# Values of two steps together and a softmax in three parts, in a four-layer attention kernel

## The reference

```python
x = L0(x)   # channel attention: h = group_norm(x); q,k,v = W h + b; softmax(q k^T / sqrt(32)) v; x + proj
x = L1(x)   # one head over points: softmax(q^T k), value with 128 channels; x + gamma * Wo y
x = L2(x)   # 8 heads of 32 over 1024 points: h = group_norm(x); softmax(q^T k / sqrt(32)) v; x + proj
x = L3(x)   # the same with its own weights; the residual is the normalised x
```

## Time and profile before

| | |
|---|---|
| time, median of 3 runs | 2928.32 us (2926.51 to 2933.37) |
| the profiled execution's own time | 2925.99 us |
| its span, first to last instruction | 2924.2 us |
| PE busy | 2778.9 us, 95% |
| POOL busy | 2154.3 us, 74% |
| DVE busy | 1863.7 us, 64% |
| ACT busy | 1553.3 us, 53% |
| mean granted TensorE clock | 0.987 |

### The profile page before, as it was taken

How to read it: one execution, slowest core, us unless ns; L and a number is a source line. 1 busy time by engine, 2 the same in 40 slices (tenths; PEclk the granted TensorE clock), 3 DMA queues, 4 the chain that set the end, 5 groups by cost and what they waited for, 6 DMA issues and landing times.

```text
span 2924.2 us, 35836 instructions
## 1 busy us (share of the span) xinstructions
PE 2778.9 (95%) x12912; PEld 1379.1 (47%) x12912; DVE 1863.7 (64%) x3341; ACT 1553.3 (53%) x2794; POOL 2154.3 (74%) x740
## 2 busy tenths in 40 slices
PE   6879999999999999999999999999999999999998
PEld 4444445544455444554445445454445544444442
DVE  1347776576756667566675676756776566767672
ACT  2225655556555556455564555644655446566554
POOL 3208777688867788687886888858887688887877
PEclk9979999999999999999999999999999999999999
DMA  2060344303434145232450334413343313433340
GB/s 81 25 95 18 47 75 60 51 20 47 88 46 56 24 51 93 33 52 46 53 94 13 46 60 57 76 23 35 60 74 60 48 24 46 75 46 46 46 60 16
DMA packets 74387, 150.85 MB, mean 52 GB/s; under 512 B 9121, under 2 KB 10657, under 8 KB 74210
## 3 DMA queue, kind: packets, MB, share of 16 engines
q1 hardware_dynamic: 74210, 148.56, 33.2%
HBM read 20.46 MB, written 16.78 MB: 13 GB/s over the span
## 4 chain that ended last, share of the span: by engine, by line
PE 70%; ACT 9%; POOL 8%; DMA 6%; DVE 4%; issue 3%; SPq 0%; ACTq 0%; POOLq 0%; DVEq 0%
PE psum L1335 16%; PE psum L1360 12%; PE psum L1304 11%; PE psum L1243 6%; POOL vT L841 5%; PE psum L1274 5%; ACT prob L945 5%; PE psum L1251 4%; PE psum L1356 4%; DMA K<-hi 3%; DMA Q<-max_rows 2%; PE psum L1383 2%; PE psum L1178 2%; POOL acc L841 2%; PE psum L1378 1%
## 5 line engine op out<-in xcount | busy, mean ns | idle before, releaser
L1082 DVE TENSOR_REDUCE maxpart<-psum 128x1 f32<-128x512 f32 x2176 | 1407.1, 684 | 730.2 <-PE psum L1304 705.9
L945 ACT ACTIVATE prob<-psum 128x512 f32<-128x512 f32 x2176 | 1224.8, 596 | 921.9 <-PE psum L1335 886.7
L841 POOL TENSOR_TENSOR acc<-acc,prob 128x2048 f32<-128x2048 f32 (+1 forms) x317 | 1130.3, 3566 | 163.4 <-ACT prob L945 133.9
L1335 PE MATMUL psum<-Q,K 104*128 104x512 f32 x2048 | 1080.7, 529 | 69.4 <-ACT prob L945 41.5
L1304 PE MATMUL psum<-K,Q 96*128 96x512 f32 x2048 | 820.8, 404 | 15.1 <-DVE maxpart L1082 11.6
L1335 PEld LDWEIGHTS psum<-Q,K 104*128 104x128 f32 x2048 | 384.4, 188 | 765.7 <-ACT prob L945 473.9
L841 POOL TENSOR_TENSOR vT<-vT,prob 128x2048 f32<-128x2048 f32 x122 | 556.2, 4559 | 22.5 <-ACT prob L945 12.0
L1360 PE MATMUL psum<-prob,vT 128*32 128x512 f32 x4096 | 555.6, 604 | 0.0
L1304 PEld LDWEIGHTS psum<-K,Q 96*128 96x128 f32 x2048 | 391.9, 191 | 149.3 <-issue 72.4
L841 POOL TENSOR_TENSOR acc<-prob 128x2048 f32<-128x2048 f32 (+1 forms) x58 | 212.3, 3661 | 314.7 <-ACT prob L945 161.9
L1360 PEld LDWEIGHTS psum<-prob,vT 128*32 128x32 f32 x4096 | 97.2, 108 | 197.0 <-ACT prob L945 110.3
(11 more groups left out here) (138 smaller groups left out, 2070.5 us busy)
## 6 DMA issues: line engine op xcount, KB each, us to landing
Q<-hi SPq DMA_DIRECT2D x128, 256.0 KB
K<-hi SPq DMA_DIRECT2D x128, 256.0 KB
Q<-lo SPq DMA_DIRECT2D x64, 256.0 KB
K<-lo SPq DMA_DIRECT2D x64, 256.0 KB
scratch<-xa SPq DMA_DIRECT2D x8, 1024.0 KB, 4.0
xb<-scratch SPq DMA_DIRECT2D x8, 1024.0 KB, 4.8
xa<-in_x SPq DMA_DIRECT2D x7, 1024.0 KB, 8.6
out<-hb SPq DMA_DIRECT2D x7, 1024.0 KB, 5.8
```

The source lines that it names most:

```text
L841: pool.tensor_tensor(total, first if a == 1 else total, this, ALU.add).then_inc(added, 1)
L945: act.activation(prob[STEP_STARTS.slot(b, start)][:, j, :], score_bank[(SCORES.rank[b.n][e] - 1) % SCORE_BANKS], ACT.Exp, scale=1.0 if lay ...
L1082: dve.tensor_reduce(maxpart[layer][:, a // NQ, a % NQ:a % NQ + 1], bank, AX_X, ALU.max).then_inc(max_free, 1)
L1335: pe.matmul(score_bank[(r - 1) % SCORE_BANKS], left, right, start=True, stop=True).then_inc(score_full, 1)
```

## The change

1. The values of two steps are issued together in groups 2.2, 2.3 and 3.0 of the steady turns (`PAIRED`): at the last slot of an even step the values of the two steps before, and none at the last slot of an odd step. So values come at slots 3, 11, 19 and 27.
2. A finish waits in the plan for a slot with values, and invert and scale follow it by 2 and 5 slots, as before. After a paired group's slot 3 that makes finish 11, invert 13, scale 16.
3. Layer 0's softmax is three events: `softmax0` (maximum and subtraction on DVE), `exp0` (ACT), `scale0` (the rest on DVE), each with a slot of its own. In 2.2 there are 19 events spread over slots 12 to 30 instead of 17: rows 12 and 13, turn 14 to 17, gram 18 to 24, keys 25 and 26, logits with `softmax0` 27, `exp0` 28, `scale0` 29. `maxrow` at slot 27 comes behind the logits.
4. Layer 2's out pieces in 3.0 start at slot 20 instead of 16.

```diff
+PAIRED = {(2, 2), (2, 3), (3, 0)}
...
-    return ([("side", layer, "gram"), ("side", layer, "keys"), [("side", layer, "logits"), ("softmax0", layer)]]
+    return ([("side", layer, "gram"), ("side", layer, "keys"), [("side", layer, "logits"), ("softmax0", layer)], ("exp0", layer), ("scale0", layer)]
...
-            b += spread(12, end, side(0, "rows", 2) + side(0, "turn", KC // 2) + gram_to_logits)
+            b += spread(12, end, side(0, "rows", 2) + side(0, "turn", KC // 2) + gram_to_scale)
...
-             (1, 0, spread(0, 7, rest5[1:3]), [(1, 1, 0, 8, 0, 3), rows(1, 1, 6)]),
-             (1, 1, spread(0, 6, rest5[3:6]), []),
+             (1, 0, spread(0, 7, rest5[1:4]), [(1, 1, 0, 8, 0, 3), rows(1, 1, 6)]),
+             (1, 1, spread(0, 6, rest5[4:8]), []),
...
-              + [(3, 0, paced(0, 4, late3) + spread(SCALED, end, out2),
+              + [(3, 0, paced(0, 4, late3) + spread(SCALED + 4, end + 1, out2),
...
-            pending.extend((clock + after, (kind,) + x[1:3]) for kind, after in
-                           (("finish", FINISH_AFTER), ("invert", INVERT_AFTER), ("scale", SCALE_AFTER)))
+            pending.append((clock + FINISH_AFTER, ("finish",) + x[1:3]))
+
+    def finished(of, now):
+
+        for kind, after in (("invert", INVERT_AFTER), ("scale", SCALE_AFTER)):
+            pending.append((now + after - FINISH_AFTER, (kind,) + of))
+        pending.sort(key=lambda x: x[0])
...
+                paired = groups is turns[3] and (layer, g) in PAIRED
+                with_values = j == HPT - 1 and (s % 2 == 0 or not paired)
...
-                while pending and pending[0][0] <= clock:
+                while pending and pending[0][0] <= clock and (with_values or pending[0][1][0] != "finish"):
                     x = pending.pop(0)[1]
                     (turning if x[0] == "finish" else plan).append(x)
+                    if x[0] == "finish":
+                        finished(x[1:], clock)
...
-                while j == HPT - 1 and len(late) > LAG:
+                while with_values and len(late) > LAG:
                     advance(plan)
...
-    OWN = {"stats": 1, "norm": 1, "softmax0": 4, "split": 3, "invert": 1}
+    OWN = {"stats": 1, "norm": 1, "softmax0": 1, "scale0": 3, "split": 3, "invert": 1}
...
-                    elif e[0] == "softmax0":
-                        act.wait_ge(l0_ready, b.after(SOFTMAX0, e))
+                    elif e[0] == "exp0":
+                        act.wait_ge(l0_ready, b.after(SOFTMAX0, ("softmax0", e[1])))
...
-                        dve.wait_ge(l0_exp, b.after(SOFTMAX0, e))
+                    elif e[0] == "scale0":
+                        dve.wait_ge(l0_exp, b.after(SOFTMAX0, ("softmax0", e[1])))
```

More of the change, by code:

```diff
@@ L140, in group_sequence @@
     rest0 = channel_attention(False)
-    gram_to_logits, from_attv = rest0[:3], rest0[3:]
+    gram_to_scale, from_attv = rest0[:5], rest0[5:]
     def at(slots, pieces):
@@ L183, in group_sequence @@
     norm5, begin5, rest5 = normalise(NEXT0), channel_attention(True, NEXT0)[-2 - KC // 2:], channel_attention(False, NEXT0)
-    turn5, out5 = begin5[2:], rest5[7:]
+    turn5, out5 = begin5[2:], rest5[9:]
     image0 = channel_attention(True) + rest0
@@ L189, in group_sequence @@
                  + beside(image0[at_out:], turn5) + begin5[:2] + split_operand(1, 0) + side(1, "v", 2) + rest5[:1]),
-             (1, 0, spread(0, 7, rest5[1:3]), [(1, 1, 0, 8, 0, 3), rows(1, 1, 6)]),
-             (1, 1, spread(0, 6, rest5[3:6]), []),
-             gap(cut(rest5[6:7] + out1[:T * NQ + 7] + out5[:2] + out1[T * NQ + 7:T * NQ + 9] + out5[2:]
+             (1, 0, spread(0, 7, rest5[1:4]), [(1, 1, 0, 8, 0, 3), rows(1, 1, 6)]),
+             (1, 1, spread(0, 6, rest5[4:8]), []),
+             gap(cut(rest5[8:9] + out1[:T * NQ + 7] + out5[:2] + out1[T * NQ + 7:T * NQ + 9] + out5[2:]
                      + out1[T * NQ + 9:] + early2[:4] + v2[:2] + early2[4:6] + v2[2:] + early2[6:]) + maxima2[:8] + beside(cut(late2[:6]), maxima2[8:])
@@ L264, in advance @@
             plan.append(("evacuate",) + x[1:3])
-            pending.extend((clock + after, (kind,) + x[1:3]) for kind, after in
-                           (("finish", FINISH_AFTER), ("invert", INVERT_AFTER), ("scale", SCALE_AFTER)))
+            pending.append((clock + FINISH_AFTER, ("finish",) + x[1:3]))
[3 more added lines that the diff above has]
+        pending.sort(key=lambda x: x[0])
     turns = group_sequence()
-    for groups in turns:
+    for n, groups in enumerate(turns):
         plan = []
@@ L273, in plans @@
                 while late:
-                    advance(plan)
-                plan += [x for _, x in pending] + flat(pieces if ("max", 2, 0, 0) in pieces else cut(pieces))
-                pending.clear()
+                    if late[0][0] == "value" and late[0][3:] == (0, 0):
+                        while pending:
+                            x = pending.pop(0)[1]
+                            plan.append(x)
+                            if x[0] == "finish":
+                                finished(x[1:], clock)
+                    advance(plan)
+                while pending:
+                    x = pending.pop(0)[1]
+                    plan.append(x)
+                    if x[0] == "finish":
+                        finished(x[1:], clock)
+                plan += flat(pieces if ("max", 2, 0, 0) in pieces else cut(pieces))
                 if at + 1 < len(groups) and groups[at + 1][0] == 1:
```

## The result

| | before | after |
|---|---|---|
| time, median | 2927.41 us (8 runs) | 2945.45 us (8 runs, 2935.68 to 2954.48) |
| the profiled execution's own time | 2925.99 us | 2935.68 us |
| its span | 2924.2 us | 2933.9 us |
| its mean granted TensorE clock | 0.987 | 0.985 |
| PE, POOL busy | 2778.9, 2154.3 us | 2772.4, 2153.6 us |

The change makes the kernel slower: ratio 1.006, interval 1.0042 to 1.0078. The profiled execution is the quickest of the eight of after; over the eight, time goes roughly with the mean granted clock of TensorE, from 2935.68 us at 0.985 to 2954.48 at 0.979. "Half clock" is a stretch in which TensorE is granted 1.2 GHz and not 2.4.

A forecast was written before the change was run, and what follows sets the result against it. It took PE's issue plus short waits as the bound, with POOL's queue deciding in 3.0. Terms: -6 x 1.1 + 15.4 - 1 = +7.8 us, so 2936.1 us against the median of 2928.3; range 2916 to 2949.

The forecast's parts named there:

- the likeliest case: Whole kernel: the forecast itself, around +8 us, 2930 to 2942 us; chance 0.35.
- rival B: Much slower: same POOL wait, slot 13's bank wait and ACT's pace at their upper ends, +21 us, 2949; chance 0.15.
- The join, 0.34 us: Steady turns' 2.2, 2.3, 3.0: joining two values batches saves 0.34 us in starts, 12 joins, 4.1 us a turn.
- Slot 13's bank, 1.6: 2.2, slot 13: PE's rows 1 waits 1.6 us for the finish's side bank, freed by the later invert; range 1.2 to 1.8.
- Up to 3.0's first score, -1.1 per turn: Each steady turn before 3.0's first score: net of savings and waits is -1.1 us, range -2.4 to +0.4.
- (b): 2.2 and 2.3, slots with only score and maximum: PE waits for ACT, 1.8 us a turn, range 1.0 to 3.0.
- ACT's 29.0 us for the subtraction: Layer 0's softmax: ACT's idle time for DVE goes, -0.7 us per turn; keys beside logits cost +0.3.
- POOL's queue in 3.0, 15.4 us: 3.0: late invert and scale delay POOL's adds, so PE's finish waits; 15.4 us over six turns, range 8 to 19.
- Rival A: Faster: POOL's chain in 3.0 doesn't decide; -7 us, 2921, or -15, 2913, with small waits; chance 0.22.
- The out pieces of layer 2 ... still come after the scale: 3.0: these pieces, moved to slots 20 to 30, still follow the scale at 1284.9; no cost was given.
- TensorE's clock: 3.0 of turn 8: the granted clock of 0.96 adds 1.7 us.
- First turn, -1: First turn: two more softmaxes of this kind gain -1 us together, range 0 to -2.

The follow-up runs named there:

- split_only: Changed kernel with no group paired; softmax still in three parts, layer 2's out pieces still at slot 20; 2939.98 us.
- split_out16: Changed kernel with no group paired and layer 2's out pieces in 3.0 again from slot 16, softmax in three parts; 2930.17 us.
- out18: Changed kernel with layer 2's four out pieces in 3.0 spread from slot 18 to 30 instead of 20 to 31; 2949.73 us.
- out18_pe: As out18, and in the steady turns' 3.0 PE sums the last step's probabilities itself, so POOL does six adds, not seven; 2935.0 us.
- finish7: Changed kernel with the finish at slot 7 again (invert 9, scale 12), values still paired; 2929.51 us.
- rows14: Changed kernel with layer 0's 19 events of group 2.2 spread over slots 14 to 30 instead of 12 to 30; 2944.53 us.
- no30_early: Changed kernel with finish at slot 7, layer 2's out pieces from slot 16, and only 2.2 and 2.3 paired, not 3.0; 2914.79 us.

## Why the prediction was right, and where it was not

Slower by over 0.2% was right, and 2945.45 lies in the range, but it is 9 us above the forecast and outside the likeliest case's own 2930 to 2942, between it and rival B's 2949, whose reason (the bank and ACT's pace at their upper ends) did not hold. That the profiled pair differs by 9.7 us and the sum said 7.8 is luck: turns 3 to 8 were to take 8.8 us more and took 19.7, and the first and the last turns gave 10 back by their clock. By its steps:

- **The join, 0.34 us.** Right: 1.85 from a joined batch to the next score.
- **Slot 13's bank, 1.6.** Right: 1.47.
- **Up to 3.0's first score, -1.1 per turn.** Right where the clock stays full: -1.2 in turn 4. The terms of (b) were not measured one by one.
- **ACT's 29.0 us for the subtraction.** Gone as forecast, but the value put on it, 0.7 us a turn less 0.3, did not come in the unpaired kernel: 2.2 takes 49.8 us in `split_only` and `split_out16`, 0.1 more than before, and 2.3 the same 52.2. Beside the pairing the same wait costs 4 us a turn on the average (2122.1 - 2098.2 = 24 us in turns 3 to 8 of the profiles, 25 between the medians): 1.0 in 2.2 and the rest as half clock in 2.3.
- **POOL's queue in 3.0, 15.4 us.** The mechanism was right and the term a little small: 19.0. The invert ended 20.84 us after 3.0's first score, not 20.3, add 7 at 50.3 and not 49.7, and turn 8 lost 1.2 us where the sum had 0.6. `out18` against `out18_pe` shows the chain itself. Rival A, that it doesn't decide, was wrong.
- **"The out pieces of layer 2 ... still come after the scale", costed at nothing.** This failed as a step: I looked at what the pieces wait for and not at what they cover. Their move costs 10 to 15 us where nothing else holds 3.0 (`split_only`, `finish7`). In after itself no run shows a price of its own, since POOL's chain ends 3.0 later anyway: `out18`, with the pieces at slot 18, is no quicker (2949.73).
- **TensorE's clock.** This is the term whose absence most of the missing 9 us goes with. The forecast counted it in turn 8 alone and took every other row at full clock. After has a stretch of half clock in 2.2 and another in 3.0 in each of turns 5 to 8, two in turn 3 and two in later groups, where before had two in all steady turns. Over the runs the middle of the mean granted clock is 0.987 before and between 0.980 and 0.983 after; that difference of 0.0055, of 2930 us, is 16 us, nearly the 18 us between the medians. It isn't to be added to POOL's 19, as a part of it lies in POOL's wait.
- **First turn, -1.** Not seen. Measured were -8.4 up to turn 3, but with the loss at half clock taken out both kernels take 390 us there. The clock of the first 140 us is 0.93 after and 0.90 before, and 0.84 in `split_only`, which has the same order in the first turn.

What is still open: which wait, or which sum of them, lets the clock fall, and whether a wait is the cause at all. Half clock stood behind the wait of 1.6 us at the end of 2.2 in four of six turns, behind the bank's in four of six, and behind the 0.77 us of `rows14` in four of six. The runs of one kernel differ as well: `no30_early` gave from 2901 us at 0.992 to 2924 at 0.984.

## What to carry to other kernels

Before a filler is moved, ask not only what it waits for but which wait it covers: here PE was 95% busy, and behind the thin slots that were left it paid a wait and, in many turns, a stretch at half clock that cost more than the wait. Two edits can each lose and together win (here joined batches and the split softmax), because one takes away the cover and the other the wait beneath it; so measure the square, not each alone. Where the clock moves by itself, compare the time without what half clock took, and the same stretch of the program, beside the medians: in `finish7` the order alone saves 11 us in turns 3 to 8, while its median is 0.1% over before. And keep what a longer batch drags along (finish, invert, scale) where it was: joining the values, with the split softmax, gains 0.4% with finish and out pieces at their old slots, is level within 0.1% with the finish alone put back, and loses 0.6% with both late.

## What the runs showed of the hardware

Stretches at half clock stood behind short waits of PE and cost more than the waits; that the waits cause them is likely and not shown. Behind waits of 0.93 and 0.65 us the granted clock was 0.54 for 6.8 us; behind one of 1.59 it was 0.51 for 10.25 us; behind POOL's 2.47 us, 0.67 over 4.7 us. The levels are the two of 1.2 and 2.4 GHz: the same 13 matmuls took 3.62 us and 1.88, and eight of layer 1's 5.17 and 3.70 with the slow stretch over part of them. The same wait in the same place does not always bring it: the wait of 1.41 us for slot 13's bank stood in all six turns of after, the slow stretch behind it in four, and after turn 4's 2.00 us for POOL there was none.

In the eleven kernels whose first turns have one and the same order, these took 412.4 to 428.6 us, and nearly all of the difference is time at half clock (22.2 to 37.5 us lost).
